# Attention scores from two-part float32r stacks on 64 partitions per head, and the rotation by second weights on TensorE

## The chip, the cores and the metric

One core of one Trainium2 chip runs the kernel as one launch. The metric is the device time of an execution in microseconds (us), the median over several runs.

## What is computed

The input x has 64 sequences of 64 channels by 256 positions, the context has the same shape, all in float32. Two layers follow each other, each with layer normalisation over the positions, attention, a residual sum, layer normalisation, a feed-forward part and a residual sum. There are 8 heads of 8 channels.

```python
# layer 0, attention: x @ w_in, a band of +-64 positions around each query
scores = einsum('bqhd,bkhd->bhqk', q, k) / sqrt(8)
attn = softmax(where(abs(i - j) <= 64, scores, -huge))
o = einsum('bhqk,bkhd->bqhd', attn, v) @ w_out.T + b_out
out = einsum('nit,io->not', relu(o.T) * ctx, w_ct) + b_ct
# layer 0, feed-forward: ternary weights, then a norm rescaling by tanh and a cap
# layer 1, attention: q from x, k and v from ctx, rotary positions, all 256 keys
q, k = rotary(Wq x + bq), rotary(Wk ctx + bk)
out = Wo (softmax(q k / sqrt(8)) v) + bo
# rotary(t) = t * cos(pos) + concat(-t[4:8], t[0:4]) * sin(pos)
# layer 1, feed-forward: 4-bit weights plus low-rank terms, relu between
```

## The kernel before

**Tiling.** Two sequences fill the 128 partitions, so there are 32 pairs and 16 heads per pair. x stays in SBUF throughout (X). Each attention layer is a software pipeline over pairs (`iterations`, L235), with a ring of 3 buffers (RING). Iteration r of each engine walks over 16 steps h. In it, the scores of head h of pair r+1 and the shifted scores of head h of pair r are computed, q and k of pair r+3 are projected, values of pair r+2 are made, and pair r-1 is finished. The order is written out by hand, per engine, as `if h == ...` lines (TensorE L522 to 553, ScalarE L761 to 790, VectorE L1085 to 1107, GpSimd L1254 to 1270, SyncE L369 to 374). Semaphores alone tie the engines together. Two PSUM banks, A and B, serve jobs in a fixed order (JOBS, L56): projections, transposes of heads and of maxima, and the output projections.

**Scores in bf16 parts.** An 8-channel head product in float32 accuracy is made from bf16 operands: q and k are each split into three bf16 parts, and all nine products of a part of q with a part of k are summed by contracting over 9 x 8 = 72 rows of a stack, Qs and Ks (128 partitions, 3 ring slots, 16 heads, 256 positions). ScalarE writes the high part (L699 or L704). In layer 0 VectorE writes the rest (L1041) and GpSimd splits it into the middle and low part (L1205, L1208). In layer 1 GpSimd sums the rotation (L1216, L1221), subtracts (L1201) and splits (L1205, L1208). SyncE copies the parts into the stacks (L341, L344, 64 KB each) and then replicates them inside the stacks (L355, L357).

**A head.** `score_head` (L408) multiplies 96 rows of Qs, as the stationary operand, with Ks, in two halves of 128 queries, over 192 keys each in layer 0 and 256 in layer 1. In layer 0 a bf16 matmul of the identity with the band (L418, 384 columns, all 128 rows) goes first into the same bank and adds -1e30 outside the band. VectorE takes the maximum of each row (L1031). The maxima of 8 heads are split into three bf16 parts (`split_max`, L925; on VectorE in layer 0, on GpSimd in layer 1), transposed on TensorE (`turn_max`, L490), copied out by ScalarE (L741) and put by SyncE (`shift_rows`, L361) into rows 96 to 98 of Qs, where Ks holds a negative constant. `shifted_head` (L426) then computes the transposed scores, keys by queries, with the maximum taken off, over all 128 rows; ScalarE applies exp (L687); in layer 0 GpSimd zeroes what is outside the band (L1234, four selects for four heads). Every fourth step a values group (L459) multiplies the probabilities of four heads with V in float32: 128 rows by 32 columns each, the four heads side by side in the columns of the array.

**Projections.** `project` (L465) multiplies float32 weights with 256 columns; a float32 matmul shows as two instructions in the trace. In layer 1 the rotation needs each channel's partner. The channels lie so that the partner is 64 partitions away, and ScalarE copies the two halves of the bank crosswise (`turn_rows`, L707, two activations of 64 partitions for q and two for k).

**Order and waits.** SyncE's queue runs in order: the side load, the stack copies of pair r+2, the maxima of the second half of pair r, the replications, and the maxima of the first half of pair r+1. The scores of a pair wait at step 0 for its stacks (`stack_in`, L414), the shifted ones at steps 0 and 8 for the rows of maxima (L432). A score matmul waits until the maxima of the head three before it are taken (3 banks), a shifted one until the exp of the head two before it is done (2 banks).

## Time and profile before

| | |
|---|---|
| median of 3 runs | 1431.23 us (1430.2 to 1431.35) |
| profiled execution, span on the core | 1429.4 us |
| profiled execution, own time | not given beside the span |
| TensorE busy | 1315.2 us, 92% |
| VectorE busy | 955.8 us, 67% |
| ScalarE busy | 874.6 us, 61% |
| GpSimd busy | 716.5 us, 50% |
| mean granted TensorE clock | 0.964 of full |

The span is from the first to the last instruction. PE is TensorE's matmuls, PEld its weight loads, DVE VectorE, ACT ScalarE, POOL GpSimd and SP SyncE. The stages, in us from the span's start: loads and preparation to about 100, attention of layer 0 from within that to about 590, feed-forward of layer 0 to about 680, attention of layer 1 to about 1170, feed-forward of layer 1 to the end. Ends of matmuls are modelled, so the price of one is best read from the distance between two starts.

### The profile page before, as it was taken

How to read it: one execution, taken by the hardware profiler on the slowest of the kernel's cores; microseconds unless marked ns; L12 is line 12 of the kernel's file. 1: busy time of each engine (PE TensorE's matmuls, PEld its weight loads, DVE VectorE, ACT ScalarE, POOL GpSimd, SP SyncE). 2: the span in 40 equal slices, each digit the busy share in tenths (PEclk: the TensorE clock that was granted, in tenths of full speed). 3: DMA queues.
4: the chain of work that ended last, by engine and by line, in shares of the span. 5: the costliest groups of instructions: out<-in, count | busy, mean ns of one | idle time of the engine just before them, and what ended most of it. 6: DMA issues, size and time to landing. Idle time of an engine off the chain costs nothing.

```text
span 1429.4 us, 37785 instructions
## 1 busy us (share of the span) xinstructions
PE 1315.2 (92%) x11332; PEld 910.0 (64%) x11332; DVE 955.8 (67%) x2156; ACT 874.6 (61%) x1909; POOL 716.5 (50%) x1292
## 2 busy tenths in 40 slices
PE   1999999999999998882799999999999989999998
PEld 1666777777777776571466666666666655766675
DVE  6438878787888787468888888888888872111110
ACT  1147676666666667563488888888888875122211
POOL 6336777777777776404555655656656511010000
PEclk9869999999999999995799999999999999999999
DMA  8314444444344443001434444444444410000000
GB/s 243 78 36 95 103 100 90 96 100 100 90 96 100 100 90 87 6 12 37 92 91 104 105 95 103 103 97 104 102 97 107 93 41 1 15 30 15 15 15 29
DMA packets 90797, 111.18 MB, mean 78 GB/s; under 512 B 15056, under 2 KB 82384, under 8 KB 83056
## 3 DMA queue, kind: packets, MB, share of 16 engines
q1 hardware_dynamic: 83184, 103.38, 31.9%
q10 hardware_dynamic: 7552, 7.02, 1.7%
q8 instruction: 34, 0.56, 0.2%
q14 instruction: 27, 0.22, 0.1%
HBM read 16.52 MB, written 4.19 MB: 14 GB/s over the span
## 4 chain that ended last, share of the span: by engine, by line
PE 62%; POOL 11%; issue 11%; DVE 8%; ACT 2%; ACTq 1%; DMA 1%; POOLq 1%; SPq 1%; DVEq 1%
PE bank L459 10%; PE bank L420 8%; PE bank L652 8%; PE bank L643 8%; PE bank L436 7%; PE bank L418 5%; PE bank L470 4%; DVE row_max L1031 3%; PE bank L501 3%; POOL rot L1216 2%; PE bank L614 2%; POOL Qp L1205 2%; PE bank L490 1%; POOL k_rest L1221 1%; POOL q_rest L1201 1%
## 5 line engine op out<-in xcount | busy, mean ns | idle before, releaser
L1031 DVE TENSOR_REDUCE row_max<-bank 128x2 f32<-128x384 f32 (+1 forms) x1024 | 599.6, 617 | 148.5 <-PE bank L420 146.8
L687 ACT ACTIVATE probs<-bank 128x384 f32<-128x384 f32 (+1 forms) x1024 | 534.4, 542 | 161.8 <-PE bank L436 155.0
L420 PE MATMUL bank<-Ks,Qs 96*128 96x192 bf16 (+1 forms) x2048 | 372.1, 264 | 13.5 <-DMA Ks<-Ks 8.4
L436 PE MATMUL bank<-Qs,Ks 128*128 128x192 bf16 (+1 forms) x2048 | 367.1, 261 | 13.6 <-ACT probs L687 12.5
L1234 POOL TENSOR_SCALAR_AFFINE_SELECT probs<-probs 128x256 f32<-128x256 f32 (+1 forms) x512 | 257.2, 526 | 175.1 <-ACT probs L687 156.3
L420 PEld LDWEIGHTS bank<-Ks,Qs 96*128 96x128 bf16 x2048 | 189.3, 99 | 122.8 <-issue 37.8
L459 PE MATMUL bank<-probs,V 128*32 128x192 f32 (+1 forms) x4096 | 249.0, 361 | 3.7 <-POOL probs L1234 2.4
L436 PEld LDWEIGHTS bank<-Qs,Ks 128*128 128x128 bf16 x2048 | 188.9, 98 | 40.1 <-ACT probs L687 23.9
L418 PE MATMUL bank<-band,ident 128*128 128x384 bf16 x512 | 169.2, 331 | 1.0 <-ACT out_bias L840 0.5
L459 PEld LDWEIGHTS bank<-probs,V 128*32 128x32 f32 x4096 | 107.4, 109 | 82.7 <-issue 41.8
L1171 DVE TENSOR_TENSOR X<-bank,X 128x256 f32 (+1 forms) x32 | 13.6, 425 | 184.6 <-PE bank L652 184.6
L1216 POOL TENSOR_TENSOR rot<-rot,rope 128x256 f32<-128x256 f32 x64 | 46.9, 732 | 132.1 <-ACT rot L716 132.1
L643 PE MATMUL bank<-Ks,up_w 128*128 128x512 f32 x256 | 111.8, 592 | 0.0
L1302 POOL TENSOR_TENSOR X<-X,down_b 128x256 f32 x32 | 23.1, 751 | 169.2 <-DVE xn L1006 169.2
L470 PE MATMUL bank<-xn,att_w 128*128 128x256 f32 x192 | 66.2, 431 | 37.7 <-DVE xn L1006 37.7
L733 ACT ACTIVATE heads_sb<-bank 128x512 f32<-128x512 f32 x128 | 75.6, 591 | 27.3 <-PE bank L459 27.3
L643 PEld LDWEIGHTS bank<-Ks,up_w 128*128 128x128 f32 x256 | 48.4, 190 | 56.8 <-issue 56.4
L501 PE MATMUL bank<-ident,heads_sb 128*128 128x128 f32 x512 | 77.9, 275 | 2.0 <-ACT heads_sb L733 2.0
L901 ACT ACTIVATE probs<-bank,up_b 128x512 f32<-128x512 f32 x32 | 22.0, 687 | 85.8 <-PE bank L643 85.8
L716 ACT ACTIVATE rot<-bank,att_b 64x256 f32<-64x256 f32 x128 | 60.0, 469 | 15.2 <-PE bank L470 12.1
L901 ACT ACTIVATE Qs<-bank,up_b 128x512 f32<-128x512 f32 x32 | 22.0, 687 | 76.1 <-PE bank L643 76.1
L501 PEld LDWEIGHTS bank<-ident,heads_sb 128*128 128x128 f32 x512 | 59.2, 142 | 12.3 <-issue 4.4
(128 smaller groups left out, 1776.9 us busy)
## 6 DMA issues: line engine op xcount, KB each, us to landing
Ks<-Ks SPq DMA_DIRECT2D x64, 576.0 KB
Qs<-Qs SPq DMA_DIRECT2D x128, 192.0 KB
Qs<-Qp SPq DMA_DIRECT2D x192, 64.0 KB
Ks<-Kp SPq DMA_DIRECT2D x192, 64.0 KB
side<-in_ctx SPq DMA_DIRECT2D x64, 128.0 KB, 2.0
X<-in_x ACTq DMA_DIRECT2D x4, 1024.0 KB, 10.4
out<-X SPq DMA_DIRECT2D x8, 512.0 KB, 2.9
Qs<-max_rows SPq DMA_DIRECT2D x128, 12.0 KB
```

Of the source, the lines that this page charges most:

```text
L418: nc.tensor.matmul(dst[:, 0:2 * win], ident16[:, :], band16[:, :], start=True, stop=False)
L420: last = nc.tensor.matmul(dst[:, blk * win:(blk + 1) * win], Qs[0:SHIFT_ROW, pair[1], h, blk * P:(blk + 1) * P], Ks[0:SHIFT_ROW, pair[1], ...
L436: last = nc.tensor.matmul(dst[:, blk * win:(blk + 1) * win], Ks[:, pair[1], h, blk * P:(blk + 1) * P], Qs[:, pair[1], h, start(blk):start( ...
L459: last = nc.tensor.matmul(dst[32 * j:32 * j + 32, first:first + win], V[:, pair[1], blk, head, :], probs[:, head % 8, blk * win:(blk + 1) ...
L470: nc.tensor.matmul(job_bank[b][:, 0:T], w[:, weight, :], source, start=True, stop=True).then_inc(s[f"{b}_filled"], 1)
L501: last = nc.tensor.transpose(job_bank["A"][:, (blk * 2 + g) * P:(blk * 2 + g + 1) * P], heads_sb[:, half, g * T + blk * P:g * T + (blk + 1 ...
L643: last = nc.tensor.matmul(bank[2 + hb % 2][:, :], up_w[:, blk, hb * P:(hb + 1) * P], xT[:, cu, blk, :], start=(blk == 0), stop=(blk == 1))
L652: last = nc.tensor.matmul(bank[4 + j % 2][:, 0:T], hidden[cu][:, hb, j * P:(j + 1) * P], down_w[:, hb, :], start=(hb == 0), stop=(hb == HB ...
L687: nc.scalar.activation(probs[:, h % 8, 0:2 * win], exp_bank[h % 2][:, 0:2 * win], ACT.Exp, scale=SCALE).then_inc(s["exped"], 1)
L733: nc.scalar.activation(heads_sb[:, half, :], pv_bank[:, :], ACT.Copy).then_inc(s["heads_out"], 1)
L1031: nc.vector.tensor_reduce(row_max[:, pair[1], h, :], bank_of(pair, h)[:, 0:2 * win].rearrange("p (b k) -> p b k", b=2), AX.X, ALU.max).the ...
L1234: return nc.gpsimd.affine_select(out=part, in_=part, compare_op=ALU.is_ge, fill=0.0, base=base, pattern=[[0, 4], [-sign, width]], channel_ ...
```

## The change

Scores now come from float32r operands, float32 rounded to fewer mantissa bits. q and k are split into two parts, and four products of 8 channels take 32 rows; the layout gives each head 64 partitions, of which rows 62 and 63 carry the maxima in two parts. Even heads lie in partitions 0 to 63, odd heads in 64 to 127, so a stack has 8 slots per pair and not 16. Ks is -1 wherever nothing is copied, and Qs is 0 there.

- `score_head` uses 62 rows, `shifted_head` 64, of one half of the array. The shifted head of step i is head i ^ 1, so it lies in the half opposite to the score head of the same step. The band matmul stays as it is.
- SyncE copies each part twice, straight to its places (8 copies of 128 KB per pair); the replication inside the stacks goes. The maxima take two DMAs per half in place of one.
- VectorE (layer 0) writes the low part itself; GpSimd's splits go in layer 0, and in layer 1 one subtraction is left of three operations per projection.
- `split_max` has two operations, not four, and runs on GpSimd in both layers; the transpose of the maxima is in float32.
- In layer 1 q and k are projected a second time with rotated weights into the other half of the bank, and `turn_rows` is one activation of 128 partitions.
- Some scratch tiles of the feed-forward stages lie in other buffers.

```diff
-PARTS = 3
-SPLIT_ROWS = PARTS * PARTS * HD
-SHIFT_ROW = 96
+PARTS = 2
+SLOTS = HPP // 2
+GROUP = P // 2
+ROWS_D = GROUP // HD
+SHIFT_ROW = GROUP - PARTS
...
+            def spread(tensor, u, product, part):
+                dst = bass.AP(tensor, u * SLOTS * T + product * row, [[ROWS_D * row, 2 * HD], [T, SLOTS], [1, T]])
+                return e.dma_start(dst, part)
...
                 for i in range(PARTS):
-                    e.dma_start(Ks[COPY_ROW + i * HD:COPY_ROW + (i + 1) * HD, u, :, :],
-                                Kp[:, u, i, :]).then_inc(s[f"k_in{u}"], 16)
...
+                    for j in range(PARTS):
+                        spread(q_stack, u, i * PARTS + j, Qp[:, u, i, :]).then_inc(s[f"q_in{u}"], 16)
+                if l == 0:
+                    wait_apart(e, job_wait(s, l, "B", "k", pair, "read"))
+                else:
+                    e.wait_ge(s["k_parts"], num(pair) + 1)
+                for i in range(PARTS):
+                    for j in range(PARTS):
+                        spread(k_stack, u, i * PARTS + j, Kp[:, u, j, :]).then_inc(s[f"k_in{u}"], 16)
...
+                for odd in range(2):
+                    first = odd * GROUP + SHIFT_ROW
+                    e.dma_start(Qs[first:first + PARTS, pair[1], half * SLOTS // 2:(half + 1) * SLOTS // 2, :]
+                                .bitcast(fp32),
+                                max_rows[odd * PARTS * HEADS:(odd + 1) * PARTS * HEADS, half, :]
+                                ).then_inc(s[f"max_in{half}"], 16)
...
                 if l == 0:
                     nc.tensor.matmul(dst[:, 0:2 * win], ident16[:, :], band16[:, :], start=True, stop=False)
+                rows = slice(h % 2 * GROUP, h % 2 * GROUP + SHIFT_ROW)
                 for blk in range(2):
                     last = nc.tensor.matmul(dst[:, blk * win:(blk + 1) * win],
-                                            Qs[0:SHIFT_ROW, pair[1], h, blk * P:(blk + 1) * P],
-                                            Ks[0:SHIFT_ROW, pair[1], h, start(blk):start(blk) + win],
+                                            Qs[rows, pair[1], h // 2, blk * P:(blk + 1) * P],
+                                            Ks[rows, pair[1], h // 2, start(blk):start(blk) + win],
...
+            def shifted_head(pair, i):
...
+                n = num(pair) * HPP + i
+                h = i ^ 1
...
+                dst = exp_bank[i % 2]
+                rows = slice(h % 2 * GROUP, h % 2 * GROUP + GROUP)
                 for blk in range(2):
                     last = nc.tensor.matmul(dst[:, blk * win:(blk + 1) * win],
-                                            Ks[:, pair[1], h, blk * P:(blk + 1) * P],
-                                            Qs[:, pair[1], h, start(blk):start(blk) + win],
+                                            Ks[rows, pair[1], h // 2, blk * P:(blk + 1) * P],
+                                            Qs[rows, pair[1], h // 2, start(blk):start(blk) + win],
...
+                if turned is not None:
+                    nc.tensor.matmul(job_bank[b][:, T:2 * T], w[:, turned, :], source, start=True, stop=True)
...
-                half = P // 2
-                for here, there in ((slice(0, half), slice(half, P)), (slice(half, P), slice(0, half))):
-                    nc.scalar.activation(rot[here, 2 * n + 1, :], job_bank[bk][there, 0:T], ACT.Identity,
-                                         bias=b[there, column:column + 1]).then_inc(s["turned"], 1)
+                nc.scalar.activation(rot[:, 2 * n + 1, :], job_bank[bk][:, T:2 * T], ACT.Identity,
+                                     bias=b[:, column:column + 1]).then_inc(s["turned"], 1)
...
+            engine.tensor_scalar(parts[:, :, 0, :].bitcast(fp32r), src, 1.0, None, ALU.mult).then_inc(high, 1)
+            wait_apart(e, (high, num(pair) + 1))
+            engine.tensor_tensor(parts[:, :, 1, :], src, parts[:, :, 0, :],
                                  ALU.subtract).then_inc(s[f"max_parts{half}"], 1)
...
                 if l == 0:
+                    split_max(e, nc.gpsimd, s, l, r, 1)
                     mask_group(m1, 3)
                     mask_group(r, 0)
-                    split("q", p3, Qp, q_rest, "q_mid", "q_parts")
                     mask_group(r, 1)
-                    split("k", p3, Kp, k_rest, "k_mid", "k_parts")
+                    split_max(e, nc.gpsimd, s, l, p1, 0)
                     gate(m1)
                     mask_group(r, 2)
```

## Rows read from the trace of the kernel before

**Rows 1.** The page's first part: busy us, share of the span, instructions.

```profile
PE 1315.2 (92%) x11332; PEld 910.0 (64%) x11332; DVE 955.8 (67%) x2156; ACT 874.6 (61%) x1909; POOL 716.5 (50%) x1292
```

**Rows 2.** Busy time by window, one window of each attention stage; PEclk is the granted clock.

```profile
200.00:500.00 300.00, 292.44 (x3178) 215.49 (x3175) 240.61 (x625) 206.47 (x471) 220.83 (x396) 1.00 0.43 97
750.00:1100.00 350.00, 343.16 (x3454) 229.88 (x3450) 303.89 (x576) 299.20 (x645) 208.31 (x414) 1.00 0.46 101
```

**Rows 3.** Waits in 200 to 500 us: total us, times, longest.

```profile
DVE row_max L1031 <- PE bank L420: 41.6, 56, 1.0
...
PE bank L490 <- DVE max_parts L941: 7.6, 19, 0.4
```

**Rows 4.** Waits in 750 to 1100 us.

```profile
PE bank L490 <- POOL max_parts L941: 6.8, 23, 0.3
...
PEld bank L459 <- ACT probs L687: 4.8, 23, 0.2
```

**Rows 5.** TensorE's timeline, layer 0: start us, us, engine, line, operation, count.

```profile
430.43 0.32 PE L418 MATMUL bank<-band,ident 128*128 128x384 bf16 x1
...
430.92 0.32 PE L418 MATMUL bank<-band,ident 128*128 128x384 bf16 x1
431.08 0.33 PE L420 MATMUL bank<-Ks,Qs 96*128 96x192 bf16 x2
431.25 0.33 PE L436 MATMUL bank<-Qs,Ks 128*128 128x192 bf16 x2
431.51 0.86 PE L459 MATMUL bank<-probs,V 128*32 128x192 f32 x16
432.30 0.44 PE L512 MATMUL bank<-ident,normed 128*128 128x128 f32 x2
432.57 0.61 PE L479 MATMUL bank<-att_w,xn 128*128 128x128 f32 x4
```

**Rows 6.** The same timeline at two f32 projections.

```profile
424.91 0.62 PE L470 MATMUL bank<-xn,att_w 128*128 128x256 f32 x2
425.37 0.33 PE L418 MATMUL bank<-band,ident 128*128 128x384 bf16 x1
...
428.46 0.70 PE L470 MATMUL bank<-xn,att_w 128*128 128x256 f32 x2
429.00 0.33 PE L418 MATMUL bank<-band,ident 128*128 128x384 bf16 x1
```

**Rows 7.** TensorE's timeline, layer 1.

```profile
905.05 0.38 PE L420 MATMUL bank<-Ks,Qs 96*128 96x256 bf16 x2
905.27 0.38 PE L436 MATMUL bank<-Qs,Ks 128*128 128x256 bf16 x2
905.58 1.07 PE L459 MATMUL bank<-probs,V 128*32 128x256 f32 x16
906.58 0.39 PE L420 MATMUL bank<-Ks,Qs 96*128 96x256 bf16 x2
...
907.03 0.38 PE L512 MATMUL bank<-ident,normed 128*128 128x128 f32 x2
907.25 0.61 PE L479 MATMUL bank<-att_w,side 128*128 128x128 f32 x4
```

**Rows 8.** SyncE's timeline, layer 0.

```profile
423.78 2.03 SPq L341 DMA_DIRECT2D Qs<-Qp  x3
...
427.92 0.77 SPq L366 DMA_DIRECT2D Qs<-max_rows  x1
```

**Rows 9.** Groups by shape, 200 to 500 us: count | busy us, mean ns.

```profile
L1031 DVE TENSOR_REDUCE row_max<-bank 128x2 f32<-128x384 f32 x302 | 157.4, 552 | 41.6 <-PE bank L420 41.6
...
L1205 POOL TENSOR_SCALAR Qp<-q_rest 128x256 bf16<-128x256 f32 x19 | 16.1, 848 | 0.0
```

**Rows 10.** Groups by shape, 750 to 1100 us.

```profile
L1031 DVE TENSOR_REDUCE row_max<-bank 128x2 f32<-128x512 f32 x369 | 240.0, 683 | 18.1 <-PE bank L420 17.6
...
L716 ACT ACTIVATE rot<-bank,att_b 64x256 f32<-64x256 f32 x93 | 43.6, 469 | 2.3
```

More of the change, by code:

```diff
@@ L80, in build @@
     i32 = mybir.dt.int32
+    fp32r = mybir.dt.float32r
     ALU = mybir.AluOpType
@@ L159, in build @@
         down_f = ff[:, 3 * FF // P:4 * FF // P, :].rearrange("p (a b) t -> p a (b t)", a=2)
-        hidden = [Qs[:, 0:2, :, :].rearrange("p a h t -> p (a h t)").bitcast(fp32)
-                  .rearrange("p (h t) -> p h t", h=FF // P), probs]
+        hidden = [ff[:, n * 2 * FF // P:(n + 1) * 2 * FF // P, :].rearrange("p a t -> p (a t)")
+                  .rearrange("p (h t) -> p h t", h=FF // P) for n in range(2)]
         bank = [stack.enter_context(nc.psum_tensor(f"bank{n}", [P, 512], fp32)) for n in range(8)]
@@ L166, in build @@
         job_bank = {"A": bank[6], "B": bank[7]}
-        max_bank = {b: job_bank[b][0:PARTS * HPP, 0:P // 2].bitcast(bf16) for b in "AB"}
+        max_bank = {b: job_bank[b][0:2 * PARTS * HEADS, 0:P] for b in "AB"}
         passed = sem("passed")
@@ L463, in values_group, with project @@
                 last.then_inc(s["pv_done"], 1)
-            def project(b, name, pair, weight, source, wait):
+            def project(b, name, pair, weight, source, wait, turned=None):
                 if not active(pair):
@@ L489, in turn_max @@
                         (s[f"max_parts{half}"], num(pair) + 1))
-                nc.tensor.transpose(max_bank[b], max_parts[:, half, :, :].rearrange("p n h -> p (n h)"),
-                                    ident16[:, :]).then_inc(s[f"{b}_filled"], 1)
+                nc.tensor.transpose(max_bank[b], max_parts[:, half, :, :, :].rearrange("p o n h -> p (o n h)"),
+                                    ident[:, :]).then_inc(s[f"{b}_filled"], 1)
             def turn_heads(pair, half):
@@ L739, in max_out @@
                 wait_job(e, s, l, bk, f"max{half}", pair, "filled")
-                wait_some(e, s[f"max_in{half}"], num(pair) * 16)
+                wait_some(e, s[f"max_in{half}"], num(pair) * ROWS_IN)
                 nc.scalar.activation(max_rows[:, half, :], max_bank[bk], ACT.Copy).then_inc(s[f"{bk}_read"], 1)
@@ L1030, in maximum, with rest_of @@
                 e.wait_ge(s["scored"], num(pair) * HPP + h + 1)
-                nc.vector.tensor_reduce(row_max[:, pair[1], h, :],
+                nc.vector.tensor_reduce(row_max[:, pair[1], h // HEADS, h % 2, h % HEADS // 2 * 2:h % HEADS // 2 * 2 + 2],
                                         bank_of(pair, h)[:, 0:2 * win].rearrange("p (b k) -> p b k", b=2),
                                         AX.X, ALU.max).then_inc(s["maxed"], 1)
-            def rest_of(bk, name, pair, parts, rest, column):
+            def rest_of(bk, name, pair, parts, column):
                 if not active(pair):
@@ L1039, in rest_of @@
                 e.wait_ge(s[f"{name}_high"], num(pair) + 1)
-                wait_some(e, s[f"{name}_parts"], num(pair) - RING + 1)
-                nc.vector.scalar_tensor_tensor(out=rest[:, pair[1], :], in0=job_bank[bk][:, 0:T],
+                nc.vector.scalar_tensor_tensor(out=parts[:, pair[1], 1, :], in0=job_bank[bk][:, 0:T],
                                                scalar=b[:, column:column + 1], in1=parts[:, pair[1], 0, :],
@@ L1187, in pool_attention, with low_part @@
             s = L[l]
-            def split(name, pair, parts, rest, mid, done):
+            def low_part(name, pair, parts, rest):
                 if not active(pair):
```

178 lines of the change are left out of this document (67 added, 111 removed).

## The prediction

> **What bounds the kernel now.** I read the shares of the page first, then the two attention stages in windows, then who waited for whom, and last TensorE's timeline instruction by instruction, since a share cannot say what a matmul costs. TensorE is busy for 92% of the span, the others for 50 to 67% [rows 1]. In a stretch of each attention stage it is busy for 292.4 of 300 us and 343.2 of 350 us at the full granted clock, 2.4 GHz [rows 2]; there are 302 and 369 score heads in them, 16 per pair, so a pair takes 15.9 us in layer 0 and 15.2 us in layer 1 [rows 9, 10], and the 32 pairs of both make some 995 of the 1429.4 us. In layer 0 VectorE waits for TensorE's scores for 41.6 us, while TensorE waits for the split maxima for only 7.6 us, 0.4 us per pair [rows 3]. In layer 1 the waits of TensorE that the view gives are about as small, 6.8 and 4.8 us over 23 pairs, and VectorE, at 303.9 of 350 us, is close behind it [rows 2, 4]. So TensorE's own order of instructions sets both stages, and I cost the change there.
>
> **Prices on TensorE.** A layer-0 head takes 0.49 us: band matmul (384 columns) 0.16, two score matmuls 0.17, two shifted ones 0.17, each of 192 columns thus 0.083 [rows 5]. A layer-1 head takes four of 256 columns, 0.22 per two, 0.11 each [rows 7]. All bf16 streams, with their weight loads hidden. The only group in another array shape is the values group (128 rows x 32 columns): from the last pair of shifted matmuls to it pass 0.26 us instead of 0.17 [rows 5], and 0.31 instead of 0.22 in layer 1 [rows 7]: **0.09 us for a change of shape**. Behind it: layer 1's group takes 1.00, layer 0's 0.79; the 0.21 between them are 64 columns in four rounds, 0.82 ns per column and round, so 192 columns in four rounds are 0.63 and 0.16 are left for staggered starts and the way out. I take 0.09 for that too, the entry being the cleaner row, and keep 0.14 as the upper bound. After such a change the first weight load is no longer hidden: the same two f32 projection matmuls take 0.54 us behind a values group and 0.46 elsewhere, +0.08 [rows 6]; two f32 transposes take 0.27 against 0.22, +0.05 [rows 5, 7]. Sixteen f32 matmuls fit in four rounds, so tiles of the array do run side by side where they differ in columns.
>
> **The change on TensorE, layer 0, per pair.** The new score and shifted matmuls use 62 or 64 rows in opposite halves of the array; no row of before shows row halves, nor float32r. Lowest price of a float32r column: the bf16 one, highest: the f32 one. I take bf16's, the stack being meant as one pass over rounded operands.
> - Overlap: the second score matmul and the first shifted one are neighbours in opposite halves; the second shifted one shares its half with the first, and the next head's scores too. One stream in four disappears: 16 x (0.083 - 0.01) = -1.2 us. If halves don't overlap, 0.
> - Shape: the band matmul still uses all 128 rows, and stands ahead of every head. Each head has one change from it to the 64-row shape (16) and one back to what follows, except where a values group followed already (4) or a maximum transpose behind one (1): 11. 27 x 0.09 = +2.4 us. Bound: 0, if row halves need no change, to 27 x 0.14 = 3.8.
> - Loads exposed behind them: 16 one-pass loads of 0.05, plus q, out and mix at 0.08 and the transposes at step 5 at 0.05: +1.1 us. Bounds: 0 and 1.6 (all at 0.08).
> - Maxima: two operations instead of four, on GpSimd; half of TensorE's 0.4 us goes: -0.2.
> Sum +2.1 us, x 32 = **+68 us**.
>
> The trace shows the 0.09 for a change of columns alone. The Trainium skill, "TensorEngine Tiling (Array Packing)", section "Tiling Modes", says that changing the tiling mode, and not just the tile, drains the array, so rows as well as columns. By it the +2.4 stands; by the trace alone it could be 0, which is the first rival.
>
> **Layer 1, per pair.** Overlap 16 x (0.11 - 0.01) = -1.6. Between heads stand five blocks in the full shape that touched no change before (steps 1, 5, 8, 10, 14): 10 changes x 0.09 = +0.9 (upper 1.4). Exposed loads: 10 entries at 0.05, three projections at 0.08, two transposes at 0.05: +0.84. Second weights: two f32 projections, each two instructions of 256 columns at 0.82 ns, 4 x 0.21 = +0.86, fully on the path. ScalarE's half-tile copies (469 ns each [rows 10]) go from four to two per pair, 0.94 us, off the path; with the shorter GpSimd chain I let 0.3 us of TensorE's waits go. Sum +0.7, x 32 = **+22 us**.
>
> **What lies beside.** GpSimd loses four split operations per pair in layer 0 (848 ns for one [rows 9]), VectorE its eight on maxima: cover for nothing, as neither is the bound. The new order puts the split of the second half's maxima ahead of the first mask; it waits for row_max of head 15, so the mask and the values group of step 3 come about 0.5 us later. The longer heads hide it here; with shorter ones it costs up to 0.5. SyncE: 8 copies in place of 6 plus 3 replications, at 0.67 us each (three in 2.03) [rows 8], and 2 issues for each half's maxima in place of 1 (0.77 each). The second half's rows, issued at 427.92 before, now stand behind 8 copies: 423.78 + 8 x 0.67 + 2 x 0.77 = 430.7 for the issue; the first use is in step 8, behind the transposes and projections that start at 432.30 and 432.57 [rows 5]. That leaves some 2 us for the landing, and more with longer heads: nothing, with 0 to 0.7 us per pair if it comes late. The memory start loses one memset off the path, and the feed-forward stages only get other buffers: nothing, either way under 3 us.
>
> **Sum.** The page's execution has a span of 1429.4 us; its own time is not given, and the median of the runs, 1431.2, lies 1.8 above, which I take as what lies around the span. 1429.4 + 68 + 22 + 1.8 = **1521 us**. This case's own range: up by the upper shape price (37 x 0.05 x 32 = +59) and loads (+25) to 1605, down to 1480 if overlap in the neighbouring pairs is better than I count.
>
> **Rivals.**
> 1. Faster: the row halves cost no change of shape, and so expose no loads. Then layer 0 saves 1.4 per pair, layer 1 1.6 + 0.3 - 0.86 = 1.0, but VectorE works 13.2 of the then 14.2 us there (303.9 us over 23 pairs [rows 2, 10]), so I count half: 1.9 x 32 = 61, **1370 us** (1350 to 1400). For it: an instruction with 96 rows follows and precedes ones with 128 rows at no price now [rows 5]; against it: those may count as one shape, and every row with another tile size pays 0.09. It decides where the cost of a change, load included, falls under 2.4 / 37 = 0.066 us; I forecast 5.3 / 37 = 0.14.
> 2. Slower still, no overlap: the halves run one after the other, shape prices as forecast: +(1.2 + 1.6) x 32 = +90, **1611 us**. Against it: the side-by-side columns of the values group.
> 3. float32r streams at f32's 0.82 ns per column, not 0.43: three streams per head, 16 x 3 x 0.075 = 3.6 and 16 x 3 x 0.10 = 4.8 us, x 32 = +270, **about 1790 us**. For it: every 4-byte stream in the trace goes at that rate. Against it: those split their operands into two parts, which the rounding here is to spare.
> 4. The change gives nothing that shows: gains and shape costs meet at the break-even of rival 1, 1431.
>
> **How the numbers follow.** Forecast 0.46, rival 1 0.31, rival 2 0.10, rival 3 0.09, rival 4 0.04. Within 0.2% (2.9 us), which is about what this measurement can tell from none, lies rival 4 alone. Faster 0.31, same 0.04, slower 0.65. Range 1360 to 1620: it holds the forecast, rival 1 and rival 2 but for their ends, and leaves out rival 3 and about 0.08 of tails. The forecast's own range is 1480 to 1605.
>
> **What would show it.** In TensorE's timeline: a head of layer 0 at about 0.64 us (0.49 before), with 0.25 or more from band to first score matmul where 0.16 stood; in layer 1 heads at 0.34 with a gap on both sides of every projection; first shifted matmul within 0.02 us of the second score one. Busy share of VectorE down in layer 0, periods of 18.0 and 15.9 us per pair. Wrong would be: heads of 0.42 (rival 1), no near-simultaneous starts (rival 2), streams 0.16 apart in layer 0 (rival 3), or a wait of the shifted matmul of step 8 on the copied rows.

## Result and the profile after

The kernel after takes **1528.9 us** (median of 4 runs, 1527.2 to 1532.7) against 1430.7 (4 runs, 1427.5 to 1431.4) before: 1.069 times as long, with a 95% interval of 1.067 to 1.071. The forecast was 1521 us, slower. The profiled execution took 1529.45 us, its span is 1527.6.

The page's first part, after:

```profile
PE 1437.3 (94%) x11460; PEld 911.7 (60%) x11460; DVE 899.9 (59%) x1900; ACT 847.9 (56%) x1845; POOL 524.2 (34%) x1035
```

Against [rows 1] TensorE gained 122 us of busy time, while GpSimd lost 192, VectorE 56 and ScalarE 27. All of that relief lies on engines that did not set the end. In the tables and lines below, a head is the two score matmuls and the two shifted matmuls of one step, with the band matmul in layer 0.

To see where the time went, I cut both spans at ScalarE's exps. A period is the time from every sixteenth exp to the next, the median over the settled part of a layer.

| stretch, us | before | after | difference |
|---|---|---|---|
| start to first exp | 90.8 | 108.6 | +17.8 |
| exps of layer 0 | 506.4 | 581.3 | +74.9 |
| to the first exp of layer 1 | 97.1 | 95.9 | -1.2 |
| exps of layer 1 | 496.7 | 503.4 | +6.7 |
| last exp to the end | 238.4 | 238.4 | 0 |
| period, layer 0 | 15.89 | 17.98 | +2.09 |
| period, layer 1 | 15.22 | 15.31 | +0.09 |
| first two periods, layer 0 | 17.6, 14.9 | 27.3, 17.7 | +12.5 |

Of the 74.9 us of layer 0, 30 settled periods at 2.09 make 63, and the first two 12.5. The windows of after (columns: stretch, its length, busy us of TensorE, weight loads, VectorE, ScalarE and GpSimd, granted clock, DMA share, GB/s) answer to [rows 2]:

```profile
200.00:500.00 300.00, 297.62 (x2803) 178.57 (x2802) 187.65 (x415) 185.31 (x417) 160.45 (x350) 1.00 0.25 69
850.00:1100.00 250.00, 249.66 (x2507) 161.43 (x2508) 212.54 (x408) 196.34 (x425) 87.39 (x163) 1.00 0.29 78
```

In this stretch of layer 0 TensorE is busy throughout at 2.4 GHz and issues 2803 matmuls where it issued 3178: each matmul got dearer. The DMA share fell from 0.43 to 0.25, which bought nothing. TensorE's timeline of after, layer 0 (start us, duration, engine, line, operation, rows*columns of the array, shape, count), beside [rows 5]:

```profile
400.10 0.33 PE L418 MATMUL bank<-band,ident 128*128 128x384 bf16 x1
400.36 0.35 PE L421 MATMUL bank<-Ks,Qs 62*128 62x192 f32 x1
400.37 0.35 PE L439 MATMUL bank<-Qs,Ks 64*128 64x192 f32 x1
400.55 0.27 PE L421 MATMUL bank<-Ks,Qs 62*128 62x192 f32 x1
400.56 0.27 PE L439 MATMUL bank<-Qs,Ks 64*128 64x192 f32 x1
400.76 0.34 PE L418 MATMUL bank<-band,ident 128*128 128x384 bf16 x1
401.03 0.35 PE L421 MATMUL bank<-Ks,Qs 62*128 62x192 f32 x1
```

A head takes 0.66 us, 0.49 before. From the band to the first score matmul pass 0.26 us, 0.16 before. The first shifted matmul starts within 0.01 us of the first score one, although the program issues both score matmuls ahead of it, and the two second ones start together 0.19 us later. From there to the next band pass 0.20 (0.08 before). Layer 1, beside [rows 7]:

```profile
1000.54 0.38 PE L421 MATMUL bank<-Ks,Qs 62*128 62x256 f32 x1
1000.55 0.38 PE L439 MATMUL bank<-Qs,Ks 64*128 64x256 f32 x1
1000.77 0.28 PE L421 MATMUL bank<-Ks,Qs 62*128 62x256 f32 x1
1000.77 0.39 PE L439 MATMUL bank<-Qs,Ks 64*128 64x256 f32 x2
...
1001.01 0.27 PE L421 MATMUL bank<-Ks,Qs 62*128 62x256 f32 x1
1001.22 1.07 PE L462 MATMUL bank<-probs,V 128*32 128x256 f32 x16
```

Without a band between them two heads take 0.68 us, 0.34 each, the way out to the values group included (0.44 before, without it). Here the halves pay. The waits of after (total us, times, longest) in 200 to 550 us, where [rows 3] stood:

```profile
DVE row_max L1032 <- PE bank L421: 111.6, 117, 1.6
...
PEld bank L462 <- POOL probs L1218: 5.8, 19, 0.4
```

and in 800 to 1200 us, where [rows 4] stood:

```profile
DVE row_max L1032 <- PE bank L421: 42.0, 104, 2.4
PEld bank L421 <- DVE row_max L1032: 29.3, 76, 0.4
...
PEld bank L439 <- ACT probs L694: 6.2, 24, 2.4
```

Layer 0 is TensorE's but for one wait a pair: VectorE waits for it for 111.6 us of 350, and the values group of step 3 starts 0.41 us behind the last shifted matmul, 0.20 elsewhere, because GpSimd's mask now comes later.

In layer 1 the view puts 29.3 us of idle time of the weight loads down to VectorE's maxima. That is no lost time. The first score matmul behind a values group starts 0.31 us after the group's last start where the view names VectorE and 0.31 where it says "issue", as it did before the change: the gap is the change of shape, and the maxima do not lengthen it. The chain of work from 900 to 1050 us is TensorE's alone:

```profile
by line: PE bank L421 30.3%; PE bank L462 26.0%; PE bank L439 11.0%; PE bank L475 9.5%; PE bank L474 8.4%; PE bank L506 6.8%; PE bank L484 3.0%; PE bank L495 2.7%; PE bank L517 2.5%
```

So layer 1 is TensorE's as well. The one wait of it that costs time is for ScalarE's exp, 0.24 us a pair (6.2 us, 24 times), with a weight load exposed behind it.

### The profile page after: what moved, and what is told of

Same layout as the page of the kernel before. It is cut to its first block, busy times and chain, and to the rows that moved or that the text cites. A ratio compares the mean times of both kernels' runs of the same rounds, so it can differ in the third digit from the quotient of the medians.

```text
span 1527.6 us, 37239 instructions
## 1 busy us (share of the span) xinstructions
PE 1437.3 (94%) x11460; PEld 911.7 (60%) x11460; DVE 899.9 (59%) x1900; ACT 847.9 (56%) x1845; POOL 524.2 (34%) x1035
## 4 chain that ended last, share of the span: by engine, by line
PE 85%; DVE 4%; POOL 4%; issue 2%; ACT 2%; ACTq 1%; SPq 1%; DMA 0%; POOLq 0%; DVEq 0%
PE bank L421 21%; PE bank L462 14%; PE bank L475 7%; PE bank L658 7%; PE bank L649 7%; PE bank L418 6%; PE bank L506 4%; PE bank L439 4%; POOL probs L1218 3%; PE bank L474 3%; PE bank L484 2%; PE bank L620 2%; PE bank L495 1%; PE bank L517 1%; DVE row_max L1032 1%
## 5 line engine op out<-in xcount | busy, mean ns | idle before, releaser
L439 PE MATMUL bank<-Qs,Ks 64*128 64x192 f32 (+1 forms) x2048 | 459.3, 319 | 10.2 <-ACT probs L694 9.1
L421 PE MATMUL bank<-Ks,Qs 62*128 62x192 f32 (+1 forms) x2048 | 460.6, 321 | 7.3 <-DVE row_max L1032 7.1
L421 PEld LDWEIGHTS bank<-Ks,Qs 62*128 62x128 f32 x2048 | 304.6, 193 | 220.4 <-issue 164.6
L439 PEld LDWEIGHTS bank<-Qs,Ks 64*128 64x128 f32 x2048 | 297.9, 189 | 22.0 <-ACT probs L694 17.8
L462 PEld LDWEIGHTS bank<-probs,V 128*32 128x32 f32 x4096 | 108.3, 110 | 72.1 <-POOL probs L1218 8.2
L940 POOL TENSOR_SCALAR max_parts<-row_max 128x16 fp32r<-128x16 f32 x128 | 32.5, 254 | 341.7 <-DVE row_max L1032 334.7
L906 ACT ACTIVATE ff<-bank,up_b 128x512 f32<-128x512 f32 x64 | 44.0, 687 | 161.8 <-PE bank L649 161.8
L658 PE MATMUL bank<-down_w,ff 128*128 128x256 f32 x512 | 112.6, 381 | 0.8 <-ACT ff L906 0.8
L649 PE MATMUL bank<-probs,up_w 128*128 128x512 f32 x256 | 111.8, 593 | 0.0
L658 PEld LDWEIGHTS bank<-down_w,ff 128*128 128x128 f32 x512 | 96.6, 190 | 15.8 <-ACT ff L906 1.6
L649 PEld LDWEIGHTS bank<-probs,up_w 128*128 128x128 f32 x256 | 48.4, 190 | 56.8 <-issue 56.4
## 6 DMA issues: line engine op xcount, KB each, us to landing
ff<-in_down_q ACTq DMA_DIRECT2D x1, 1024.0 KB, 10.5
```

The source lines that it names most:

```text
L421: last = nc.tensor.matmul(dst[:, blk * win:(blk + 1) * win], Qs[rows, pair[1], h // 2, blk * P:(blk + 1) * P], Ks[rows, pair[1], h // 2, s ...
L439: last = nc.tensor.matmul(dst[:, blk * win:(blk + 1) * win], Ks[rows, pair[1], h // 2, blk * P:(blk + 1) * P], Qs[rows, pair[1], h // 2, s ...
L462: last = nc.tensor.matmul(dst[32 * j:32 * j + 32, first:first + win], V[:, pair[1], blk, head, :], probs[:, head % 8, blk * win:(blk + 1) ...
L649: last = nc.tensor.matmul(bank[2 + hb % 2][:, :], up_w[:, blk, hb * P:(hb + 1) * P], xT[:, cu, blk, :], start=(blk == 0), stop=(blk == 1))
L658: last = nc.tensor.matmul(bank[4 + j % 2][:, 0:T], hidden[cu][:, hb, j * P:(j + 1) * P], down_w[:, hb, :], start=(hb == 0), stop=(hb == HB ...
```

## Experiments

The theory was that row halves overlap and that the shape changes and float32r weight loads around them cost more. The rivals were no overlap, a price of the rows alone that is nil, and causes outside TensorE. Each run stands against the kernel before on the same chip (1430.5, 1429.7 and 1429.9 us in the three sets). Four executions of one kernel lie up to 21 us apart (E5, 1520 to 1542), so the periods say more than the totals where these differ by 10 us or less.

| kernel | us (runs) | period layer 0 | layer 1 | to first exp |
|---|---|---|---|---|
| e1, both in one half | 1672.8 (1) | 21.27 | 16.19 | 110.0 |
| e2, two-part stacks, all rows | 1506.6 (1) | 17.28 | 16.33 | 94.9 |
| e3, bf16, 64 rows for scores | 1609.1 (1) | 18.73 | 17.51 | 101.2 |
| e4, bf16 in halves | 1438.5 (1) | 16.29 | 14.58 | 99.9 |
| e5, GpSimd waits | 1530.0 (4) | 18.01 | 15.32 | 107.3 |
| e6, no second weights | 1517.9 (6) | 17.99 | 15.17 | 108.3 |
| e7, after, no band | 1522.5 (4) | 19.34 | 15.30 | 99.6 |
| e8, before, no band | 1391.7 (4) | 14.68 | 15.22 | 93.1 |
| e9, bands in pairs | 1489.5 (4) | 16.88 | 15.30 | 104.8 |
| e10, filler in pair 0 | 1533.6 (4) | 17.99 | 15.31 | 107.8 |
| e11, e4 without band | 1381.5 (1) | 14.54 | 14.65 | 93.4 |

**E1: is there overlap?** In `shifted_head` and `exp_head` of after:

```diff
-                h = i ^ 1
+                h = i
```

> The changed kernel, with the shifted head taken in natural order, so that it lies in the same half of the array as the score head of its step. Theory (halves run side by side, two streams of four are hidden): every head of layer 0 is longer by two streams of 0.083 to 0.107 us, 0.17 to 0.21, that is 2.7 to 3.4 us per pair and 85 to 110 us in all; layer 1 by up to 0.22 per head, less what TensorE idles there now, 60 to 110 us. Sum 1670 to 1750 us. Rival (the simultaneous starts are only how the trace shows them): about 1529 us.

1672.8 us, 144 more than after. Two lines of its timeline in layer 0:

```profile
402.01 0.46 PE L421 MATMUL bank<-Ks,Qs 62*128 62x192 f32 x2
402.32 0.38 PE L439 MATMUL bank<-Qs,Ks 64*128 64x192 f32 x2
```

In layer 0 the near-simultaneous starts are gone: two score matmuls run in one half, then two shifted ones. A head takes 0.88 us, 0.22 more than in after, which is two starts of 0.11. The overlap is real, and two matmuls of four are hidden by it, worth 3.3 us per pair in layer 0. The 0.9 us in layer 1 is no such price: where no band stands between two heads, the scores of the next head lie in the opposite half and still start beside this head's (at 1102.24 and 1102.26 us). Consecutive float32r matmuls of 192 columns in one half start 0.11 us apart, where bf16 ones do at 0.083.

**E2: the stacks without halves.** After, with all 128 rows for both kinds of matmul:

```diff
-                rows = slice(h % 2 * GROUP, h % 2 * GROUP + SHIFT_ROW)
+                rows = slice(0, P)
...
-                rows = slice(h % 2 * GROUP, h % 2 * GROUP + GROUP)
+                rows = slice(0, P)
...
-                                     scale=SCALE).then_inc(s["exped"], 1)
+                                     scale=SCALE * 1e-30).then_inc(s["exped"], 1)
```

> The changed kernel, with score and shifted matmuls over all 128 partitions of the float32r stacks: products of two heads are summed, and the exp has a scale near zero, so the output is not the reference's; operands, loads and columns per matmul stay. No change of array shape around heads, and no halves. Theory (the shape changes and the loads exposed behind them are the cost): no gap around the band matmul, a layer-0 head of 0.49 to 0.59 us, depending on whether a weight load of 0.107 us limits a stream of 0.083; layer 0 at 16 to 17.6 us per pair against 18.0, layer 1 at 16.0 against 15.3 (second weights, four streams again). 1450 to 1540 us. Rival (float32r itself is what costs): layer 0 loses the overlap on top, 20 us or more per pair, 1600 us or more.

1506.6 us. Its timeline in layer 0:

```profile
401.00 0.34 PE L418 MATMUL bank<-band,ident 128*128 128x384 bf16 x1
401.04 0.50 PE L421 MATMUL bank<-Ks,Qs 128*128 128x192 f32 x2
401.37 0.39 PE L439 MATMUL bank<-Qs,Ks 128*128 128x192 f32 x2
```

There is no change of shape around the heads, and still a head takes 0.60 us against 0.49: with float32r stacks and all rows, layer 0 takes 1.4 us more per pair than before, by weight loads that no longer hide behind 192 columns. In layer 1 it takes 1.1 more, of which the second weights are 0.86. And the halves, which should pay for themselves, lose on balance: after is 22 us slower than this kernel. They give 1.0 us per pair back in layer 1, cost 0.7 in layer 0, 13.7 us ahead of the first exp and 10.5 in the first two periods (45.0 us together in after, 34.5 here). The start alone is thus as large as the whole difference.

**E3: the price of rows alone.** The kernel before, with the scores on 64 rows (an incomplete sum of products) and the shifted ones on 128:

```diff
-                                            Qs[0:SHIFT_ROW, pair[1], h, blk * P:(blk + 1) * P],
-                                            Ks[0:SHIFT_ROW, pair[1], h, start(blk):start(blk) + win],
+                                            Qs[0:64, pair[1], h, blk * P:(blk + 1) * P],
+                                            Ks[0:64, pair[1], h, start(blk):start(blk) + win],
```

> The kernel before, with the score matmuls over rows 0 to 63 of its bf16 stacks instead of 0 to 95 (part of the products is left out of the scores that give the maxima), the shifted ones unchanged over 128 rows. Nothing but the array shape of one matmul pair per head changes. Theory (a change between 128 rows and 64 rows costs 0.09 to 0.12 us, as to and from 32 columns): two more changes per head in both layers, 16 x 2 x 0.1 = 3.2 us per pair, x 64 = 205 us, 1600 to 1680 us. Rival (row halves need no change of shape): 1431 us.

1609.1 us, 179 more, with less to multiply. Its timeline in layer 0:

```profile
400.25 0.33 PE L418 MATMUL bank<-band,ident 128*128 128x384 bf16 x1
400.50 0.34 PE L420 MATMUL bank<-Ks,Qs 64*128 64x192 bf16 x2
400.77 0.34 PE L436 MATMUL bank<-Qs,Ks 128*128 128x192 bf16 x2
```

Band to score 0.25 where 0.16 stood, score to shifted 0.27 where 0.17 stood. Over the layer's starts the means rose by 0.096 and 0.093 us, in layer 1 by 0.093 and 0.096: a change of rows costs what a change of columns does. Rival 1's condition, no price for row halves, fell here. The Trainium skill, "TensorEngine Tiling (Array Packing)", section "Tiling Modes", states that changing the tiling mode drains the array. This trace agrees, in that each change costs 0.09 us.

**E4: halves without float32r.** As E3, but the shifted matmuls take rows 64 to 127 alone (again sums that lack rows):

```diff
-                                            Ks[:, pair[1], h, blk * P:(blk + 1) * P],
-                                            Qs[:, pair[1], h, start(blk):start(blk) + win],
+                                            Ks[64:P, pair[1], h, blk * P:(blk + 1) * P],
+                                            Qs[64:P, pair[1], h, start(blk):start(blk) + win],
```

> The kernel before, with the score matmuls over rows 0 to 63 and the shifted ones over rows 64 to 127 of its bf16 stacks (part of the products is left out of both). It has the shapes and the overlap of the changed kernel, but bf16's loads and no second weights. Theory (shape changes cost 0.1 each, bf16 loads next to nothing): layer 0 per pair -16 x 0.166 + 27 x 0.1 = 0, layer 1 -16 x 0.22 + 10 x 0.1 = -2.5 on TensorE, where VectorE's 13.2 us then bind at 14 to 14.5. 1390 to 1440 us. Rival (the load is not what makes the changed kernel's heads long): layer 0 at about 18 us per pair as in the changed kernel, 1480 us or more.

1438.5 us. Its timeline in layer 0:

```profile
401.52 0.33 PE L418 MATMUL bank<-band,ident 128*128 128x384 bf16 x1
401.78 0.25 PE L420 MATMUL bank<-Ks,Qs 64*128 64x192 bf16 x1
401.78 0.25 PE L436 MATMUL bank<-Qs,Ks 64*128 64x192 bf16 x1
401.87 0.24 PE L420 MATMUL bank<-Ks,Qs 64*128 64x192 bf16 x1
401.88 0.24 PE L436 MATMUL bank<-Qs,Ks 64*128 64x192 bf16 x1
402.05 0.34 PE L418 MATMUL bank<-band,ident 128*128 128x384 bf16 x1
```

The head of 0.53 us is two changes of shape and two hidden streams. The second pair follows after 0.09 us, not 0.19, so the weight load that stands exposed in after is float32r's. The loads themselves say the same: the second score load starts 0.01 to 0.02 us behind the first here and is recorded with 0.09 us, in after it starts 0.107 behind and is recorded with 0.18. Of after's 98 us over before, 8 are left. The kernel differs from after in more than the operands: 55 of the 90 lie in the exps of layer 0, where the operands' type is the main difference, 26 in those of layer 1, where the second weights are gone too, and 9 ahead of the first exp.

**E5: the start, GpSimd.** In after VectorE's normalisation of the first pair runs beside a dequantisation on GpSimd. VectorE's and GpSimd's timelines of after:

```profile
22.34 4.21 DVE L1007 TENSOR_SCALAR xn<-X,mean,rstd 128x256 f32<-128x256 f32 x1
```

```profile
21.04 5.37 POOL L924 TENSOR_SCALAR ff<-ff 128x2048 f32<-128x2048 int32 x1 [12.09 <-DMA probs<-in_lora_out]
```

The same VectorE instruction took 0.41 us before, when GpSimd had nothing there. The edit moves GpSimd's work behind it:

```diff
+            e.wait_ge(L[0]["xn_ready"], 2)
             dequantise(e, nc.gpsimd, up_f, up_raw,
```

> The changed kernel, with GpSimd's first dequantisation held until the first two normalised inputs are written. Theory (at the start VectorE's first normalisation took 4.2 us, and 0.4 before, because GpSimd's dequantisation now runs beside it; TensorE began 4.3 us later for it): first projection at 22.4 us again, 4 us less, about 1525 us. The rest of the 17.8 us by which the first exp comes later is the half clock, which stays low to 136 us and is not changed by this. Rival (the start moves, but the preparation that TensorE waits for next ends no earlier): 1529 us, same.

1530.0 us (ratio to before 1.068, 1.060 to 1.076): no gain that its spread could show. The VectorE instruction took 0.41 us again, the first projection came 3.5 us earlier, and the first exp only 1.3. GpSimd's work beside it is what stretched the instruction, and it is not the cause of the late start.

**E6: the second weights.** After, without the turned matmuls (`turn_rows` reads the first half of the bank, so the rotation gets the wrong partners):

```diff
-                if turned is not None:
+                if False:
...
-                nc.scalar.activation(rot[:, 2 * n + 1, :], job_bank[bk][:, T:2 * T], ACT.Identity,
+                nc.scalar.activation(rot[:, 2 * n + 1, :], job_bank[bk][:, 0:T], ACT.Identity,
```

> The changed kernel without the two second projections of layer 1; the rotation's partner rows are read from the first projection instead, so that the rotation is wrong, with ScalarE's work unchanged. Theory (TensorE sets layer 1): 0.86 us less per pair, 28 us less, 1501 us. Rival (VectorE sets layer 1 now, with 13.2 us of work in a period of 15.3 us and TensorE waiting 1.1 us per pair for it): at most 0.3 us per pair, 1520 to 1529 us.

1517.9 us (ratio 1.060, 1.057 to 1.064), 11 less than after by the medians. Its profiled execution, the slowest of six, gained 5.6 us in the exps of layer 1, 0.14 per period in the settled part, and as a whole none (span 1527.9). With 0.86 us per pair off the path it would have been 27. The expectation's rival came near the time for a wrong reason: it is not VectorE that takes over. Waits in 800 to 1200 us, and the chain from 900 to 1050:

```profile
PEld bank L421 <- DVE row_max L1032: 30.8, 79, 0.8
...
PEld bank L439 <- DMA Qs<-max_rows: 5.0, 15, 1.1
```

```profile
by line: PE bank L421 22.5%; SPq L334 19.2%; PE bank L462 18.7%; PE bank L439 10.1%; DMA Qs<-max_rows 7.8%; PE bank L475 7.5%; PE bank L506 5.1%; SPq L364 2.7%; issue 2.3%; PE bank L495 2.0%; PE bank L517 1.0%; PE bank L484 0.9%; SPq L283 0
```

The first line is as in after and costs nothing here either. The second is the new one: the shifted matmuls of step 8 wait for the copied rows of maxima, which stand in SyncE's queue behind the eight stack copies (0.6 us each) and land 1.95 us after their issue. That queue, absent from the chain of after, is 30% of it here with the landings, and takes back what the second weights gave. In after itself the second weights lie on the path in full.

**E7: after without the band.** If band and shape changes make the layer-0 head long, heads without a band should take what layer 1's take. Left out is the matmul that adds the band; the maximum is then over the whole window, and the mask of GpSimd still zeroes what is outside:

```diff
-                if l == 0:
-                    nc.tensor.matmul(dst[:, 0:2 * win], ident16[:, :], band16[:, :], start=True, stop=False)
...
-                                            start=(l == 1), stop=(l == 1 or blk == 1))
+                                            start=True, stop=True)
```

> The changed kernel without the band matmul of layer 0: the maximum is then taken over the whole window of 192 keys and not over the band within it; the masks after the exp still remove what is outside. Theory (the full-height matmul between the halves costs its columns, two changes of shape and an exposed load, 0.43 of a head's 0.66 us): TensorE needs 11 us per pair, VectorE's 11.3 bind, layer 0 at 12 to 13 us per pair, 1340 to 1375 us, and the start no slower than that. Rival (halves and float32r are slow by themselves): only the 0.16 us of its columns go, 16 x 0.16 x 32 = 82 us, 1447 us.

1522.5 us (ratio 1.065, 1.058 to 1.072). A miss, by some 150 us. Pairs that fall wholly into full clock take 14.4 to 15.6 us, with heads at 0.22 where they follow each other, so even these are 2 us above the forecast of 12 to 13. And the clock does not stay full. Windows of it:

```profile
200.00:500.00 300.00, 272.24 (x2509) 181.82 (x2509) 178.95 (x412) 172.24 (x412) 157.66 (x346) 0.82 0.24 65
285.00:302.00 17.00, 16.78 (x141) 11.19 (x141) 8.78 (x21) 8.82 (x20) 7.31 (x16) 0.70 0.15 40
319.00:336.00 17.00, 15.27 (x175) 10.47 (x177) 11.87 (x29) 11.05 (x28) 10.11 (x23) 1.00 0.27 72
```

The granted clock alternates between 2.4 and 1.2 GHz through layer 0: some 231 of the 583 us of its exps are at 1.2 GHz, where after has 38 of 581 (the time ahead of the first clock record counted as 1.2 GHz, as the durations show it), and what the shorter heads saved is lost to it.

**E8: before without the band.** The same edit in the kernel before.

> The kernel before without its band matmul, as the other side of the comparison; the maximum is over the window here too. Only the 384 columns go: 0.16 x 16 = 2.6 us per pair, TensorE at 13.3 and VectorE at 12.8 us, so 13.4 to 13.8 per pair, 1350 to 1367 us. If layer 0 were set by another engine than TensorE: 1400 us or more.

**1391.7 us, ratio 0.974 (0.971 to 0.977)**: faster than both kernels. Less was gained than expected (1350 to 1367 us), 1.2 us per pair of the 2.6 that 16 band matmuls take. Windows 200 to 500 us and waits there:

```profile
200.00:500.00 300.00, 274.36 (x3109) 200.57 (x3107) 251.13 (x676) 210.40 (x512) 236.28 (x429) 1.00 0.47 105
```

```profile
PEld bank L488 <- issue: 23.1, 41, 0.8
...
PE bank L488 <- DVE max_parts L939: 12.8, 21, 0.6
```

The clock stays full, and the next limit comes up: TensorE waits for split maxima, and VectorE is at 251 of 300 us. The band's removal asks of the data that no score outside the band exceeds the row's maximum inside it by so much that exp loses the row.

**E9: fewer changes of shape.** After, with the bands of heads h and h+1 issued together at even h, so that the second head's matmuls follow the first's in halves:

```diff
-                if l == 0:
+                if l == 0 and h % 2 == 0:
                     nc.tensor.matmul(dst[:, 0:2 * win], ident16[:, :], band16[:, :], start=True, stop=False)
+                    wait_some(e, s["maxed"], n + 1 - SCORE_BANKS + 1)
+                    nc.tensor.matmul(bank_of(pair, h + 1)[:, 0:2 * win], ident16[:, :], band16[:, :],
+                                     start=True, stop=False)
```

> The changed kernel, with the band matmuls of two heads issued one behind the other ahead of the even head, where the bank of the odd head is free early enough. Same columns, fewer changes of shape: five odd heads per pair (7, 9, 11, 13, 15), ahead of which stands no other full-height job, lose a way out and a way in and an exposed load, 0.12 + 0.10 + 0.11 less what stays as a stream, 0.25 to 0.3 us each, 1.3 to 1.5 us per pair, 40 to 48 us. Theory: 1480 to 1490 us, layer 0 at 16.6 per pair. Rival (the clock pays it back, as in the run without the band, where it fell to half in four tenths of the time): the granted clock falls in layer 0 and the time stays at 1500 us or above.

1489.5 us (ratio 1.041, 1.039 to 1.043). The same arithmetic in another order gives back 39 of the 98 us, some 34 by the period of layer 0 and 4 ahead of the first exp. Its timeline:

```profile
301.05 0.35 PE L424 MATMUL bank<-Ks,Qs 62*128 62x192 f32 x1
301.06 0.35 PE L442 MATMUL bank<-Qs,Ks 64*128 64x192 f32 x1
301.25 0.27 PE L424 MATMUL bank<-Ks,Qs 62*128 62x192 f32 x1
301.25 0.38 PE L442 MATMUL bank<-Qs,Ks 64*128 64x192 f32 x2
301.37 0.27 PE L424 MATMUL bank<-Ks,Qs 62*128 62x192 f32 x1
```

The second head enters 0.11 us behind the first's last matmuls, where 0.20 to the band and 0.26 behind it stood. The clock stayed at 2.4 GHz in the window of 200 to 500 us: E7's alternation did not come with the bands in pairs.

**E10: the clock at the start.** Before, the clock is recorded as full from 49.3 to 59.5 us, in the heads that fill pair 0, and falls again. After, it rises for the first time at 136.5, and the head at 109.48 us takes 1.14 us instead of 0.66:

```profile
109.48 0.53 PE L418 MATMUL bank<-band,ident 128*128 128x384 bf16 x1
109.94 0.53 PE L421 MATMUL bank<-Ks,Qs 62*128 62x192 f32 x1
...
110.62 0.50 PE L418 MATMUL bank<-band,ident 128*128 128x384 bf16 x1
```

The edit gives pair 0 two more band matmuls ahead of each score head, overwritten by what follows:

```diff
+                if l == 0 and isinstance(pair[0], int) and num(pair) == 0:
+                    for _ in range(2):
+                        nc.tensor.matmul(dst[:, 0:2 * win], ident16[:, :], band16[:, :], start=True, stop=True)
```

> The changed kernel with two more band matmuls ahead of each score head of pair 0 alone (overwritten by the third; 32 matmuls of 384 columns, 5 to 10 us of work). Theory (the clock stays at 1.2 GHz until 136 us because the heads of pair 0, without shifted ones beside them, keep one half of the array only partly busy; before it rose at 49 us among those heads): the clock rises in these heads, the first exp comes no later than now in spite of the added work, and the first pairs no longer take 27.3 and 17.7 us; 1512 to 1524 us. Rival (the low start is the preparation's, whose f32 matmuls are the same in both kernels): clock low until 136 us or longer, and 5 to 10 us more, 1534 to 1540 us.

1533.6 us (ratio 1.071, 1.067 to 1.074): nothing won. Windows of it:

```profile
61.00:75.00 14.00, 14.00 (x73) 8.01 (x71) 8.89 (x20) 0.65 (x2) 0.95 (x4) 1.00 0.20 55
76.00:100.00 24.00, 24.00 (x68) 16.53 (x67) 0.00 (x0) 2.98 (x5) 0.00 (x0) 0.50 0.04 11
100.00:140.00 40.00, 39.49 (x200) 22.25 (x199) 14.51 (x34) 17.55 (x35) 9.45 (x22) 0.50 0.12 31
```

The clock did rise among the filled heads of pair 0, fell in the preparation of the feed-forward weights, and stayed at 1.2 GHz in the first two pairs, 27.3 and 20.9 us long. (In after the profile prints 1.00 for these stretches, since its first clock record is the rise at 136.5; the durations above show the lower level.)

**E11: what makes the clock fall.** E4 without the band, bf16 halves and no full-height matmul in the heads.

> The kernel before with bf16 scores over rows 0 to 63 and shifted ones over rows 64 to 127 (part of the products is left out of both), and without the band matmul. It tells whether it is the halves or float32r that let the clock fall when the band is gone. Theory (the halves; heads of two hidden streams leave too little of the array at work): granted clock under 0.9 in layer 0, its period over 15 us, 1390 us or more. Rival (float32r): clock 1.0 in layer 0, VectorE's 12.8 us bind at about 13.5, layer 1 at 14.6 as in the run with the band, 1330 to 1350 us.

1381.5 us in one run. Its window:

```profile
200.00:500.00 300.00, 255.36 (x3140) 146.69 (x3140) 250.96 (x679) 212.02 (x517) 239.03 (x432) 1.00 0.48 106
```

The clock is full although TensorE is busy for less of the time than in E7 (255 against 272 us). The theory, that halves alone bring it down, fell. But float32r halves alone do not either: in layer 1 of after they run with no band between them, 256 columns each and TensorE busy for 249.7 of 250 us, and the clock is full. The time, some 30 us above the rival's upper end of 1350, is no sign of TensorE's heads: VectorE, at 251 of 300 us, holds the period at 14.5.

## Why the prediction was right, and where it was not

The sign, the time within 8 us of 1529 and the mechanism held: overlap in halves, paid for with shape changes and exposed loads. How near the time came is luck. The period of 18.0 us in layer 0 came out as forecast, but the overlap under it was twice as large and the loads and shapes dearer, and these cancel. In the total, layer 1 came out 15 us cheaper than forecast, and the start and the first two pairs 30 us dearer.

- **Overlap, layer 0: -1.2 forecast, -2.7 found.** "The second score matmul and the first shifted one are neighbours" took the order of the program for the order of starts. The first two start together, and the second two: two streams of four are hidden, 16 x 0.17. The sign named for it, a first shifted matmul within 0.02 us of the *second* score one, did not show.
- **Shape, layer 0: +2.4 forecast, +3.1.** The change in costs 0.10 (0.26 for 0.16), the way out 0.12 (0.20 less a stream of 0.08): 16 x 0.22 less the five exits at 0.09 that existed. The count was right, and the price of the change itself nearly: some 0.03 of the way out is float32r's, since in E2, where nothing changes shape, the band follows at 0.117 and not at 0.082, and in E4, in bf16, the way out costs 0.09. E3 shows the price without overlap or float32r.
- **Exposed loads, layer 0: +1.1 forecast, +1.9.** This is the term with the wrong size: 16 x 0.107 plus 0.24 for the three projections (0.32 us between the starts of their two matmuls where 0.24 stood). The 0.107 is what lies between the starts of two consecutive float32r loads (0.19 from one matmul to the next less a stream of 0.08), and 0.05 was forecast. E4, with bf16 halves, has none of it. In E2 layer 0 takes 1.4 us per pair more without a change of shape.
- **Waits, layer 0: -0.2 forecast, about -0.26.** The transpose of the maxima started 0.64 us behind the last shifted matmul before, 0.47 of it a wait that is gone; the 0.21 for the mask came in. "The longer heads hide it here" did not hold. With this the terms make 2.0 to 2.1, against 2.09 of the trace.
- **Overlap, layer 1: -1.6 forecast, -3.5 found.** The same step failed here: two streams are hidden, 16 x 0.22, and not one. Against it stand the second weights, +0.86 as forecast (four matmuls 0.216 us apart, in a chain that is TensorE's alone), and shape changes and exposed loads, forecast at 1.7 and by difference 2.8. Some 1.1 of that are the exposed loads of ten heads that stand behind a way in, 0.107 each, where 0.05 was taken. Waits: -0.3 forecast, nothing found, since 0.46 us for the maxima and one exp went and 0.46 for another exp came. Sum +0.1 where +0.7 was forecast. Heads at 0.34 were right, the period of 15.9 was not (15.3).
- **The start: "nothing, either way under 3 us", found +17.8, and +12.5 in the first two pairs.** I costed the fill at the rates of the settled part. It runs at 1.2 GHz in after. E2, with the same stacks and no halves, has its first exp 13.7 us earlier and a rise of the clock at 54.8 us, so most of it goes with the halves; E5 leaves 1.3 us for GpSimd's part. The other runs agree. The clock first rises at 49.3 us before, 52.0 in E8 and 54.8 in E2, whose heads have 96 or 128 rows, and at 102.5 (E11), 104.9 (E4), 114.0 (E3), 114.6 (E7), 114.7 (E9), 126.3 (E1) and 136.5 (after), which all have matmuls of 62 or 64 rows, in bf16 or float32r, in the heads that fill pair 0. Why the first rise then spreads from 102 to 144 us (E6, which is after in layer 0) stays open: E10's added matmuls brought it to 61.2 us, and it did not last.
- **DMA, SyncE's queue and the copied rows of maxima: nothing, and almost nothing was found.** From 800 to 1200 us TensorE waits once for the copied rows, 0.6 us, and the DMA share fell. But the margin is thin: with 0.86 us per pair less on TensorE it is used up, and the wait named as a sign of being wrong shows in E6.

Rival 1 fell with E3 (0.09 us per change of rows, and its deciding point was 0.066 with the load included), rival 2 with E1, rival 3 with float32r starts at 0.11 us for 192 columns, rival 4 with the time.

## What to carry over

Count shape changes of the array before cutting a matmul in halves: here each costs 0.09 to 0.10 us, a little more than a bf16 stream of 192 columns, and a full-height instruction between every two heads makes two of them. Put work of one shape together first (E9: 39 us for an order), and ask whether the odd instruction is needed (E8: 2.6% faster than before, for a bound on the data's range). Fewer rows do not make the weight load shorter: with float32r operands and 192 columns it is the load that sets the pace here (0.11 us against 0.083). A gap for which a profile names an engine may have another cause: compare it with the same gap where no engine is named (layer 1). And look for the queue that comes next before removing work (E6).

## What was not expected of the hardware

- Matmuls in opposite row halves do not start in program order: in layer 0 of after the third issued is recorded as starting 7 ns behind the first, and ahead of the second by 0.19 us. A recorded start alone would not prove it (in E2 the first score matmul is recorded 0.04 us behind the start of the band's 384 columns), but the time does: without it, in E1, a head is longer by two streams and not by one.
- The weight loads of float32r operands start 0.107 us apart, are recorded with 0.18 to 0.19 us each (bf16: 0.09 to 0.10), and limit consecutive 192-column matmuls in one half to one in 0.11 us (E1; 0.083 in bf16). It is 0.11 with all 128 rows too (E2). Layer 1's 256 columns go at 0.12 where bf16 takes 0.11.
- TensorE's clock fell to 1.2 GHz with the engine busy for 272 of 300 us (E7), and stayed at 2.4 GHz with 255 of 300 (E11). The difference between the two is the type of the operands and the engine work around it. Float32r halves of 256 columns without idle time kept it too (layer 1 of after). What decides was not found.
- VectorE's 128x256 normalisation took 4.21 us beside GpSimd's 128x2048 dequantisation and 0.41 without it (after and E5).
